# Two pairs of modulation vectors made as columns with their weights stationary, and a set of orders changed on four engines, in an fp32 adaLN attention and low-rank FFN block

## What is computed

```python
mod = (silu(c) @ wmod).reshape(6, 512)          # sa, ca, ga, sb, cb, gb
ga, gb = sign(ga) * max(|ga|, 0.25), sign(gb) * max(|gb|, 0.25)
h = layernorm(x) * (1 + ca) + sa
x = x + ga * attention(h, wq, wk, wv, wo)       # 32 heads, 8 KV heads, width 128, rotary, causal
h = layernorm(x) * (1 + cb) + sb
x = x + gb * ffn(h, W, b, A, B, gate_w, gate_b) # dense 512x512, and of 4 low-rank terms one a token
```

## Time and profile before

| | |
|---|---|
| median of 3 runs | 1097.12 us (1095.56 to 1098.68) |
| the profiled execution, its own time | 1097.11 us |
| span of its profile | 1095.3 us |
| PE / PEld / DVE / ACT / POOL busy | 96 / 80 / 71 / 58 / 47% |
| mean granted TensorE clock | 0.991 |
| instructions | 16543 |

### The profile page before, as it was taken

The page is one execution under the profiler, slowest core; times in us unless marked ns, Lnnn a source line. Parts: engine busy times, 40 slices in busy tenths (PEclk is TensorE's granted clock), DMA queues, the critical chain, the costliest instruction groups (busy, mean ns, idle before and its releaser), DMA issues.

```text
span 1095.3 us, 16543 instructions
## 1 busy us (share of the span) xinstructions
PE 1053.4 (96%) x5426; PEld 872.2 (80%) x5426; DVE 773.5 (71%) x1831; ACT 634.4 (58%) x1301; POOL 520.0 (47%) x506
## 2 busy tenths in 40 slices
PE   6999999999999999999999999999999999999997
PEld 3668878888888878887888878888787878888775
DVE  4668866688558866688657865689657875688576
ACT  5547764477437754477436754477436763577433
POOL 2535653365425653365434643455524652455244
PEclk8999999999999999999999999999999999999999
DMA  6462233132302233132312223023212224022001
GB/s 214 149 218 76 87 97 78 36 100 87 94 13 68 87 97 78 35 101 87 82 25 68 78 84 99 11 94 109 58 58 68 78 78 106 6 96 73 21 20 59
DMA packets 98285, 86.92 MB, mean 79 GB/s; under 512 B 39380, under 2 KB 84052, under 8 KB 98072
## 3 DMA queue, kind: packets, MB, share of 16 engines
q1 hardware_dynamic: 98200, 85.86, 26.4%
HBM read 59.23 MB, written 26.61 MB: 78 GB/s over the span
## 4 chain that ended last, share of the span: by engine, by line
PE 58%; DVE 12%; ACT 9%; DMA 8%; POOL 5%; issue 5%; SPq 2%; POOLq 0%; DVEq 0%; ACTq 0%
PE accumulators L705 16%; PE accumulators L675 14%; PE accumulators L690 11%; PE scores L625 9%; DMA pa_lo<-p_rows 4%; PE transposed L638 4%; DMA p_rows<-turned 3%; DVE p_large L1213 3%; ACT p_large L929 3%; DVE turned L1239 2%; PE scores L894 2%; DVE o_lo L1258 2%; POOL qc L1601 2%; DVE pb_lo L1225 1%; POOL qr L1597 1%
## 5 line engine op out<-in xcount | busy, mean ns | idle before, releaser
L1588 POOL TENSOR_SCALAR p_large<-p_large,rowinv 128x640 f32<-128x640 f32 (+3 forms) x128 | 125.3, 979 | 234.8 <-DVE rowinv L1218 234.8
L937 ACT ACTIVATE pb_hi<-transposed 128x512 fp32r<-128x512 f32 (+3 forms) x256 | 118.1, 509 | 178.6 <-PE transposed L638 178.4
L1597 POOL TENSOR_TENSOR qr<-qr,trig 128x512 f32<-128x512 f32 x80 | 106.2, 1327 | 206.8 <-ACT qr L962 206.8
L929 ACT ACTIVATE p_large<-p_large,negmax 128x640 f32<-128x640 f32 (+3 forms) x128 | 126.4, 988 | 99.3 <-DVE negmax L1213 98.2
L1225 DVE TENSOR_TENSOR pb_lo<-transposed,pb_hi 128x512 fp32r<-128x512 f32 (+3 forms) x256 | 141.8, 585 | 58.7 <-ACT pb_hi L937 58.3
L1213 DVE CUSTOM_DVE_ANT_0 p_large<-scores,mask 128x640 f32<-128x640 f32 (+3 forms) x128 | 130.0, 1016 | 18.4 <-PE scores L625 14.9
L625 PE MATMUL scores<-k_hi,q_hi 128*128 128x512 f32 (+2 forms) x384 | 139.5, 363 | 1.7 <-DVE negmax L1213 1.7
L625 PE MATMUL scores<-k_hi,q_lo 128*128 128x512 f32 (+2 forms) x384 | 131.7, 343 | 0.0
L1588 POOL TENSOR_SCALAR p_small<-p_small,rowinv 128x128 f32<-128x128 f32 (+3 forms) x128 | 97.2, 774 | 71.6 <-DVE rowinv L1218 71.6
L625 PE MATMUL scores<-k_lo,q_hi 128*128 128x512 f32 (+2 forms) x384 | 131.0, 341 | 0.0
L1601 POOL TENSOR_TENSOR qc<-qc,qr 128x512 f32<-128x512 f32 x80 | 116.6, 1458 | 6.5 <-POOL qr L1597 0.3
(11 more groups left out here) (169 smaller groups left out, 2224.4 us busy)
## 6 DMA issues: line engine op xcount, KB each, us to landing
p_rows<-turned SPq DMA_DIRECT2D x31, 640.0 KB, 2.9
pa_lo<-p_rows SPq DMA_DIRECT2D x124, 160.0 KB, 3.2
stage<-in_L_attn_wq_dram SPq DMA_DIRECT2D x32, 256.0 KB, 2.8
stage<-in_L_attn_wo_dram SPq DMA_DIRECT2D x32, 256.0 KB, 3.4
v_rows<-vt SPq DMA_DIRECT2D x32, 128.0 KB, 2.8
v_lo<-v_rows SPq DMA_DIRECT2D x32, 128.0 KB, 3.2
y<-in_L_wmod_dram SPq DMA_DIRECT2D x4, 512.0 KB, 5.6
stage<-in_L_attn_wk_dram SPq DMA_DIRECT2D x8, 256.0 KB, 2.7
```

Of the source, the lines that this page charges most:

```text
L929: nc.scalar.activation(row(i), row(i), ACT.Exp, bias=negmax[:, i:i + 1], scale=-1.0, accum_out=rowsum[:, i:i + 1]).then_inc(s_exp, 1)
L937: nc.scalar.activation(pt_of(i, part, True), src, ACT.Copy).then_inc(t_hi, 1)
L1588: nc.gpsimd.tensor_scalar(row(i), row(i), rowinv[:, i:i + 1], 1.0, ALU.mult, ALU.mult).then_inc(s_norm, 1)
L1597: nc.gpsimd.tensor_tensor(qr[:, s, :], qr[:, s, :], trig[:, 1, half * HALF:(half + 1) * HALF], ALU.mult).then_inc(r_sin, 1)
```

## The change

It has three parts.

1. **Modulation as columns.** `modulation("first")` and `modulation("second")` now make a pair of vectors directly as columns: the stationary operand is a 128x128 block of `wmod`, the moving one is the single column `silu[:, 3, k]`, 4 x 8 = 32 matmuls a pair, in plain fp32. The row products of `sa`, `ca`, `sb`, `cb`, their copies to `vt` and the 8 turning matmuls are gone. `second` moves to place 3 of head 0 in the first group; place 2 is empty there. SP waits for `second` ahead of loading the weights of both gates. DVE takes `first` after the statistics of token tile 4, ahead of those of tiles 5 to 7.
2. **`early_hi` and `early_lo`.** In heads 1 and 2 both stand ahead of `rotated_hi` and `rotated_lo`. In head 3 ACT does `exp` 7 and the swap of k half 0 first and then `early_hi`; DVE does `inverse` 7 and `times_cos` of k half 0 and then `early_lo`.
3. **`rotate` split on POOL.** For the q projection in every `back`: first instruction, `normalise` 6, second instruction, `normalise` 7, where `normalise` 6 stood behind both.

```diff
@@ fillers: group 0, head 0 @@
-        (0, 2): wo(0) + mod("sb"),
-        (0, 3): wo(1) + mod("cb"),
-        (0, 4): wo(2, 3) + mod("second") + [("q", (1, 0), 0)],
+        (0, 2): wo(0),
+        (0, 3): wo(1) + mod("second"),
+        (0, 4): wo(2, 3) + [("q", (1, 0), 0)],
@@ sync @@
-            sp.wait_ge(a_full, N.value("a", ("mod", "sb"), g0))
+            sp.wait_ge(a_full, N.value("a", ("mod", "second"), g0))
             sp.dma_start(mod_w[:, :, 0:D], wmod_v[:, :, 2 * D:3 * D]).then_inc(mod_in[1], 16)
-            sp.wait_ge(a_full, N.value("a", ("mod", "cb"), g0))
             sp.dma_start(mod_w[:, :, D:2 * D], wmod_v[:, :, 5 * D:6 * D]).then_inc(mod_in[2], 16)
@@ tensor, modulation @@
-                    for n in range(2 * KC):
-                        mm = nc.tensor.matmul(acc[:, n:n + 1], vt[0:1, n * P:(n + 1) * P], ident[0:1, 0:1],
-                                              start=True, stop=True)
+                    for k in range(KC):
+                        if m == "first":
+                            pe.wait_ge(mod_in[k], 16)
+                        elif k == 0:
+                            pe.wait_ge(mod_in[0], 32)
+                        for n in range(2 * KC):
+                            mm = nc.tensor.matmul(acc[:, n:n + 1], mod_w[:, k, n * P:(n + 1) * P], silu[:, 3, k:k + 1],
+                                                  start=(k == 0 and n == 0), stop=(k == KC - 1 and n == 2 * KC - 1))
@@ tensor, prologue @@
-            for k in range(KC):
-                pe.wait_ge(mod_in[k], 16)
-                for n, m in enumerate(("sa", "ca")):
-                    mm = nc.tensor.matmul(ACC[0:1, N.slot("a", ("mod", m), g0), :], silu[:, 3, k:k + 1],
-                                          mod_w[:, k, n * D:(n + 1) * D], start=(k == 0), stop=(k == KC - 1))
...
+            modulation("first", g0)
...
-                    if half == 0 and k == 1:
-                        modulation("first", g0)
@@ scalar, back @@
+                if h in (1, 2):
+                    early_hi(h, at)
                 rotated_hi(("q", ((h + 1) % R, 0)), at, int(last))
                 if last:
                     split_hi(("v", 0), at, 1)
-                if h:
-                    early_hi(h, at)
                 if h == 2:
                     split_hi(("wo", 2), at)
                 exp(h, 7, at)
-                if not h:
+                fill(h, 5, at, slice(0, 1) if last else slice(0, -1))
+                if h in (0, 3):
                     early_hi(h, at)
-                fill(h, 5, at, slice(0, -1))
+                if last:
+                    fill(h, 5, at, slice(1, -1))
@@ vector, back @@
+                if h in (1, 2):
+                    early_lo(h, at)
                 rotated_lo(("q", ((h + 1) % R, 0)), at, int(last))
                 if last:
                     split_lo(("v", 0), at, 1)
-                if h:
-                    early_lo(h, at)
                 adds = fillers(h, 5, at.first)[:-1] if not h else []
                 fill(h, 5, at, slice(0, min(1, len(adds))))
                 inverse(h, 7, at)
                 if h == 2:
                     split_lo(("wo", 2), at)
-                fill(h, 5, at, slice(min(1, len(adds)), -1))
+                if last:
+                    fill(h, 5, at, slice(0, 1))
+                    early_lo(h, at)
+                fill(h, 5, at, slice(1 if last else min(1, len(adds)), -1))
@@ vector, prologue @@
                 norm(x_tile(t), t, ln_var)
+                if t == KC:
+                    take_modulation("first", Group(0))
             g0 = Group(0)
-            take_modulation("first", g0)
@@ gpsimd, back @@
-                rotate(("q", ((h + 1) % R, 0)), at, int(last))
+                rotate_sin(("q", ((h + 1) % R, 0)), at, int(last))
                 normalise(h, 6, at)
+                rotate_sum(("q", ((h + 1) % R, 0)), at, int(last))
                 normalise(h, 7, at)
```

More of the change, by code:

```diff
@@ L111, in __init__ @@
         self.of = {}
-        for job in (("mod", "sa", 0), ("mod", "ca", 0), ("mod", "first", 0), ("k", 0, 0), ("q", (0, 0), 0), ("q", (0, 1), 0), ("k", 1, 0), ("v", 0, 0),
+        for job in (("mod", "first", 0), ("k", 0, 0), ("q", (0, 0), 0), ("q", (0, 1), 0), ("k", 1, 0), ("v", 0, 0),
                     ("v", 1, 0)):
@@ L557, in _ @@
             sp.dma_start(turned[:, 0:T], mask_c).then_inc(mask_in, 16)
-            sp.wait_ge(a_full, N.value("a", ("mod", "ca"), g0))
+            sp.wait_ge(a_full, N.value("a", ("mod", "first"), g0))
             sp.dma_start(mod_w, wmod_v[:, :, 3 * D:5 * D]).then_inc(mod_in[0], 16)
@@ L716, in modulation @@
                 if m in ("first", "second"):
[L717 to L720 removed]
+                    for k in range(KC):
[6 more added lines that the diff above has]
+                                                  start=(k == 0 and n == 0), stop=(k == KC - 1 and n == 2 * KC - 1))
                 else:
[L722 removed]
+                    chunk, arrived = {"ga": (0, 1), "gb": (1, 2)}[m]
                     pe.wait_ge(mod_in[arrived], 32)
[L724 to L726 removed]
+                    pe.wait_ge(silu_done, 2)
                     for k in range(KC):
[L728 to L730 removed]
+                        mm = nc.tensor.matmul(acc, vt[:, k * P:(k + 1) * P], mod_w[:, k, chunk * D:(chunk + 1) * D],
+                                              start=(k == 0), stop=(k == KC - 1))
                 mm.then_inc(a_full, 1)
@@ L1060, in _ @@
                                      scale=rstd[:, t:t + 1]).then_inc(xn_done, 1)
-                if t == 3:
-                    for n, m in enumerate(("sa", "ca")):
-                        number = N.value("a", ("mod", m), Group(0))
-                        act.wait_ge(a_full, number)
-                        nc.scalar.activation(vt[0:1, n * D:(n + 1) * D], ACC[0:1, N.slot("a", ("mod", m), Group(0)), :],
-                                             ACT.Copy).then_inc(a_taken, 1)
             act.wait_ge(a_taken, N.value("a", ("mod", "first"), g0))
@@ L1309, in take_modulation @@
                 acc = ACC[:, N.slot("a", name, at), :]
-                if m in ("sb", "cb"):
-                    dve.wait_ge(v_out, 64)
-                    c0 = 0 if m == "sb" else D
-                    nc.vector.tensor_copy(vt[0:1, c0:c0 + D], acc[0:1, :]).then_inc(a_taken, 1)
-                elif m in ("first", "second"):
+                if m in ("first", "second"):
                     r = 0 if m == "first" else 2
@@ L1340, in fill @@
                         if which == "second":
+                            dve.wait_ge(v_out, 64)
                             for k in range(KC):
@@ L1588, in normalise, with rotate_sin @@
                 nc.gpsimd.tensor_scalar(row(i), row(i), rowinv[:, i:i + 1], 1.0, ALU.mult, ALU.mult).then_inc(s_norm, 1)
-            def rotate(name, at, ahead=0):
+            def rotate_sin(name, at, ahead=0):
                 kind, which = name
@@ L1598, in rotate, with rotate_sum @@
                                         ALU.mult).then_inc(r_sin, 1)
+            def rotate_sum(name, at, ahead=0):
+                s = N.slot("r", name, at, ahead)
+                n = N.value("r", name, at, ahead)
                 need(pool, r_sin, n)
@@ L1601, in rotate @@
                 nc.gpsimd.tensor_tensor(qc[:, s, :], qc[:, s, :], qr[:, s, :], ALU.add).then_inc(r_sum, 1)
+            def rotate(name, at, ahead=0):
+                rotate_sin(name, at, ahead)
+                rotate_sum(name, at, ahead)
             def scale_wo(r, at):
```

10 lines of the change are left out of this document (removed).

## The result

| | before | changed |
|---|---|---|
| median | 1097.84 us (1095.56 to 1098.68, 4 runs) | 1110.94 us (1108.86 to 1113.3, 4 runs) |
| ratio, 95% interval | | 1.0127 [1.0099, 1.0156] |
| profiled execution, own time | 1097.11 us | 1109.08 us |

A forecast was written before the change was run, and what follows sets the result against it. It took PE's list as the bound. Terms 6.2 (prologue), 0.6 (`second`), 2.5 (head 3), 2.8 and 1.2 (head 0), 2.4 (heads 1 and 2) summed to +15.7 on 1097.11: 1112.8 us, range 1091 to 1118.

The forecast's parts named there:

- main case: Whole kernel: cold `first` and late `q_hi` make it slower, 1112.8 us, own range 1105 to 1119, chance 0.52.
- prologue: Before the attention: `first` at half clock delays DVE's statistics from tile 5 and the first `1 + ca`, +6.2 us.
- `second`: Head 0 of group 0: clock falls about half-way through its passes, 10.9 us long; transposes of tile 4 +0.6 us.
- `ga`: Head 0 of group 0: part 3's lateness meets the taking of `ga`, for which PE waits already, +1.2 us.
- head 3, seven groups: End of head 3: POOL's split makes `q_hi` 1.85 us late, `early_hi` gives 1.18 back, +2.5 us in all.
- head 0, seven groups: Head 0 of groups 1 to 7: late `q_hi` delays the bank for `wo` 6 by 0.4 us each, +2.8 us.
- heads 1 and 2: Parts 2 and 3 there: waits for `early_hi` stay, small delays of 0.1 and 0.2 us a group, +2.4 us.
- The 0.5 that I added for the clock's phase: Prologue: 0.5 us added because the later start meets the clock's rise at another point.
- Point (1): Sign in the prologue: loads of `first` 0.22 us apart, ending at about 20.4, DVE's copy to `modc` at 20.5.
- A: Rival: prologue costs nothing, as loads raise the clock or do not depend on it; 1105.8 us, chance 0.13.
- B: Rival: part 3's delays are hidden by other waits of ACT and DVE, the rest holds; 1103.9 us, chance 0.15.
- C: Rival: faster, part 2 works in head 3 as `q_hi` slips under 1.18 us; 1091.9 us, chance 0.2.

The follow-up runs named there:

- run 8: Changed kernel with six fp32 matmuls of 512 moving columns on a zeroed tile ahead of `first`: 1108.73 us, ratio 1.0113.
- run 6: Changed kernel with DVE's taking of `first` moved behind the statistics of all eight token tiles: 1109.01 us, ratio 1.011.
- run 3: Kernel before with parts 2 and 3 and the old modulation: 1105.94 us, ratio 1.0058.
- runs 1, 7: Kernel before with part 2 alone: 1089.98 us, ratio 0.9913; kernel before with part 2 in head 3 alone: 1085.57 us, ratio 0.9891.
- run 5: Changed kernel with POOL's rotation in one piece again (part 3 undone, parts 1 and 2 kept): 1095.4 us, ratio 0.9981.

## Why the prediction was right

The forecast (1112.8 us, slower) held, and the main case is the one that happened. Its terms, against the table of heads above:

| term | predicted | measured |
|---|---|---|
| prologue | +6.2 | +5.2 |
| `second` | +0.6 | +0.3 |
| `ga` | +1.2 | +1.2 |
| head 3, seven groups | +2.5 | +1.6 |
| head 0, seven groups | +2.8 | +3.9 |
| heads 1 and 2 | +2.4 | +3.0 |
| two stretches of half clock in the profile of before, none such in that of the changed kernel | not in the sum | -3.4 |
| sum | +15.7 | +11.8, in a span that grew by 12.0 |

The measured terms of the heads are the steps from one head's `exp` 0 to the next, added over groups; the stretch given back between groups 4 and 5 is taken out of head 3's and stands in the row of half clock. Without that row the sum is 15.2. Single terms are off by up to 1.1 us both ways and cancel, so that the sum came so near is in part luck.

- **Prologue.** `first` ended at 20.1 where the text had 20.4, at 0.213 a pass where it had 0.22. DVE lost 5.22, not 5.7. The 0.5 that I added for the clock's phase was not paid. Point (1) and the mechanism of the half clock hold, also by run 8; that DVE's place in the order is the whole cost does not, by run 6: with DVE free, PE's cold transposes are 1.0 us late next.
- **`second`.** The sum is right by two errors. The clock fell after 45 passes and not 30, so it took 9.2 us and not 10.9; but the q projection behind it ran wholly at half clock, 5.3 us and not 4.1, and the transposes behind that partly too (1.12 us for 0.76). Run 6 shows how much is luck: the same 64 passes took 13.65, because the clock was down before they began.
- **Head 3.** `q_hi` waits 1.95 us for POOL and not 0.16, and PE 1.66 and not 1.85: 11.6 us in sum against 10.4 before, where 12.9 was predicted. The chain is the one predicted. Against PE's scores, which start 9.26 later in this group, `q_hi` is 1.80 late (1.85 predicted), and `early_hi` out of the list gives 1.31 back (1.18 predicted: `exp` 7 started 2.37 behind `q_hi` and now 1.06). The swaps and `times_cos` are 0.49 late and not 0.67. The slightly mis-sized term is the price of `early_hi`.
- **Head 0.** Waits of 0.21 to 0.50 ahead of `wo` 6, where 0.4 was predicted, but each group loses 0.55: the first matmuls behind a wait are slower too (1.19 for four, 1.07 without).
- **Heads 1 and 2.** The waits for `pa_hi` stayed (4.3 against 4.0) as predicted. The waits at transposes 6 of head 2 (0.2 a group, 1.6 in sum) went, and others came at transposes 7 (2.7 in sum). By the steps from head to head, head 1 costs 0.09 a group and head 2 0.29, where 0.1 and 0.2 were predicted.
- **Not in the sum.** Two stretches of half clock in the profile of before, 3.4 us each and so 1.7 lost each. One begins with the v projection of head 3 of group 4. The timeline of the kernel before there, and at the same place one group earlier:

```profile
519.92 1.20 PE L690 MATMUL accumulators<-h_hi,wv_hi 128*128 128x512 f32 x4 [2.23 <-DVE qc L1266]
...
644.84 2.07 PE L690 MATMUL accumulators<-h_hi,wv_hi 128*128 128x512 f32 x4 [1.94 <-DVE qc L1266]
```

In the profile of the changed kernel the same wait is 1.66 in all groups and the clock stays up behind each. That the change made this difference is not shown: the longest wait of before, 2.23, had no fall behind it either, and of the four executions of the changed kernel the two slower ones (1112.8 and 1113.3 us) had a lower mean granted clock, 0.988 and 0.987 against 0.991. So the -3.4 belongs to this pair of profiles.
- **Rivals.** A is refuted by the 0.213 a pass of the changed kernel and by run 8, B by run 3 (1105.9, not 1098). C named the right lever with the wrong partner: `early_hi` out of head 3's list is worth 9 to 13 us (runs 1, 7), and POOL's split, which makes `q_hi` 1.80 us late where part 2 gives 1.31 back, takes it away again (run 5: 15.5).

## What to carry to other kernels

On an engine that runs a strict list, one late operand delays everything behind its first reader. So before an order on another engine makes an operand late, read what is queued behind that reader, in every stage that uses the list and not only where the wait now stands. The parts of one change are not worth the same alone and together: here part 2 is worth 9 us alone and 34 beside part 3, and the best kernel (0.9891) has it in one head alone. A matmul with one moving column costs what its weight load costs, 0.112 us at 2.4 GHz and 0.213 at 1.2 GHz here, and a stream of them did not keep the upper level in any of these runs.
